# Score and maxima operands in float32r, four tiles of 32 rows, heads 2 and 3 first in the maxima

## What is computed

```python
x = x + 0.5 * moe(layernorm(x), ...)      # 8 experts, top 2, capacity 1280, gelu
x = x + attention(layernorm(x), ...)
x = x + 0.5 * moe(layernorm(x), ...)

def attention(x):                         # B=4, S=1024, H=16, Dh=8
    q, k, v = (split(x @ w.T + b) for w, b in ((wq, bq), (wk, bk), (wv, bv)))
    scores = einsum('bhsd,bhtd->bhst', q, k) / 8 ** 0.5
    weights = softmax(where(causal, scores, -inf), axis=-1)
    return merge(einsum('bhst,bhtd->bhsd', weights, v)) @ wo.T + bo
```

## Time and profile before

| | us |
|---|---|
| time, median of 3 runs (lowest, highest) | 1033.29 (1031.57, 1038.26) |
| span of the profiled execution | 1036.6 |
| TensorE matmuls busy | 831.8 (80%) |
| VectorE busy | 601.5 (58%) |
| ScalarE busy | 523.4 (50%) |
| GpSimd busy | 489.6 (47%) |
| first mixture of experts, then the attention's prologue from | 236 |
| first score at | 289.55 |
| 16 groups of heads until about | 823 |
| last mixture of experts until the end, from | 858 |

### The profile page before, as it was taken

One profiled execution on the slowest core, in us unless ns is written; L12 is line 12 of the kernel. 1 busy time (PEld: TensorE's weight loads), 2 busy tenths in 40 slices (PEclk: granted clock), 3 DMA queues, 4 the chain that ended last, 5 costly groups with the idle time before them and its releaser, 6 DMA issues. The chain is left out here.

```text
span 1036.6 us, 18080 instructions
## 1 busy us (share of the span) xinstructions
PE 831.8 (80%) x6599; PEld 446.5 (43%) x6599; DVE 601.5 (58%) x1237; ACT 523.4 (50%) x841; POOL 489.6 (47%) x686
## 2 busy tenths in 40 slices
PE   8569999944668988888978899878887618999990
PEld 7437878742212223332333323323232316787770
DVE  7931211124767788888787977878775423334235
ACT  6323343442237776777556786566766303433330
POOL 5047455325652662646467522562224651545453
PEclk9769999986657999999799999999899758999995
DMA  7115575621451262341524224323202124423236
GB/s 204 73 26 153 148 217 145 192 63 51 130 162 66 53 189 48 89 144 43 174 76 105 99 53 152 85 65 106 53 18 79 53 63 149 130 79 97 78 136 228
DMA packets 96185, 110.81 MB, mean 107 GB/s; under 512 B 12279, under 2 KB 68763, under 8 KB 96104
## 3 DMA queue, kind: packets, MB, share of 16 engines
q1 hardware_dynamic: 84752, 88.86, 29.1%
q0 software_dynamic: 9216, 17.98, 6.8%
q10 hardware_dynamic: 2136, 2.91, 0.8%
HBM read 57.86 MB, written 52.89 MB: 107 GB/s over the span
## 5 line engine op out<-in xcount | busy, mean ns | idle before, releaser
L1903 DVE TENSOR_REDUCE m_blk<-banks 128x8 f32<-128x1024 f32 (+1 forms) x320 | 348.5, 1114 | 79.7 <-PE banks L1505 67.1
L1823 ACT ACTIVATE pt<-banks 128x1024 f32<-128x1024 f32 (+3 forms) x384 | 300.4, 811 | 145.1 <-PE banks L1489 142.7
L1537 PE MATMUL banks<-pt,vs 128*32 128x512 f32 (+3 forms) x1536 | 176.6, 534 | 7.2 <-POOL pt L2252 3.8
L1489 PE MATMUL banks<-qb,kp 64*128 64x512 bf16 (+3 forms) x768 | 132.6, 351 | 53.7 <-DVE m_blk L1903 45.2
L2252 POOL TENSOR_SCALAR_AFFINE_SELECT pt<-pt 128x512 f32<-128x512 f32 x128 | 81.6, 637 | 192.1 <-ACT pt L1823 191.7
L1505 PE MATMUL banks<-kp,qa 64*128 64x128 bf16 (+4 forms) x1152 | 126.4, 294 | 19.6 <-ACT pt L1823 11.6
L849 POOL DMA_INDIRECT xe<-xn_rows,slot_tok x80 | 79.9, 999 | 94.4 <-PE banks L1190 37.2
L675 POOL DMA_INDIRECT y_tab<-ys,ids x70 | 68.0, 972 | 81.5 <-DVE ys L635 64.5
L1106 ACT ACTIVATE he<-banks,b_up 128x512 f32<-128x512 f32 (+1 forms) x96 | 57.9, 616 | 89.9 <-PE banks L1190 89.5
L1505 PEld LDWEIGHTS banks<-kp,qa 48*128 48x128 bf16 (+1 forms) x1152 | 46.2, 99 | 130.3 <-ACT pt L1823 92.7
L585 ACT ACTIVATE hT<-banks,bfc 128x512 f32<-128x512 f32 (+1 forms) x96 | 56.3, 615 | 84.9 <-DVE bfc L607 48.8
(11 more groups left out here) (344 smaller groups left out, 1128.8 us busy)
## 6 DMA issues: line engine op xcount, KB each, us to landing
bucket<-zero SPq DMA_DIRECT2D x16, 660.0 KB
qb<-q_stack SPq DMA_DIRECT2D x32, 192.0 KB, 3.5
qa<-q_stack SPq DMA_DIRECT2D x30, 192.0 KB, 3.3
kp<-k_stack SPq DMA_DIRECT2D x30, 192.0 KB, 4.2
q_stack<-qp SPq DMA_DIRECT2D x18, 256.0 KB
k_stack<-kq SPq DMA_DIRECT2D x18, 256.0 KB
y_slots<-ye SPq DMA_DIRECT2D x16, 256.0 KB, 2.5
mid<-x SPq DMA_DIRECT2D x8, 512.0 KB, 3.6
```

Of the source, the lines that this page charges most:

```text
L1489: i = nc.tensor.matmul(ring[SLOT["score", 2 * u + pair]][:, s, 0:w], kp[g][rows_s, pair, kb * P:(kb + 1) * P], qb[par][rows_s, pair, q0:q0 ...
L1537: i = nc.tensor.matmul(o_bank[VW * h:VW * h + VW, q:q + w], vs[par][:, kb, h, :], pt[u % PTS][:, h, 0:w], start=u in (0, SECOND), stop=u i ...
L1823: nc.scalar.activation(pt[u % PTS][:, 2 * pair:2 * pair + 2, 0:w], ring[SLOT["score", 2 * u + pair]][:, :, 0:w], ACT.Exp, scale=SCALE).the ...
L1903: nc.vector.tensor_reduce(dst, ring[slot][:, :, 0:blocks * P].rearrange("p s (j k) -> p s j k", k=P), AX.X, ALU.max).then_inc(m_done, 1)
```

## The change

q and k are cut into two float32r parts instead of three bf16 parts, so three products of parts make 24 rows per head instead of 48, in words of four bytes. A head then takes a tile of 32 rows, and the four heads of a group lie on rows 0, 32, 64 and 96 (HR = 32) rather than two and two on the same rows. The second and third parts' steps go: the remainder that VectorE forms is the second part. Maxima are cut into two float32r parts in two steps by GpSimd; the rows that they meet in `kp` hold -1 rather than 1, in place of the negation. Loads of stacks and of maxima are one transfer per head (4) instead of one per 64 rows (2), stores of stacks 3 for each of q and k instead of 6. In the list of maxima units the pair of heads 2 and 3 comes ahead of heads 0 and 1, so M0 is of heads 2 and 3 and M1 of heads 0 and 1.

```diff
-    Q_PART = [0, 0, 0, 1, 1, 2]
-    K_PART = [0, 1, 2, 0, 1, 0]
+    Q_PART = [0, 0, 1]
+    K_PART = [0, 1, 0]
+    HR = 32
...
-            for pair in range(2):
+            for pair in (1, 0):
                 MUNITS.append((hf, pair, segs, row, col, False))
...
-            qa = [sba(f"qa{i}", [P, HS // 2, S], bf16) for i in range(2)]
-            qb = [sba(f"qb{i}", [P, HS // 2, S], bf16) for i in range(2)]
-            kp = [sba(f"kp{i}", [P, HS // 2, S], bf16) for i in range(NG)]
+            qa = [sba(f"qa{i}", [P, S], f32r) for i in range(2)]
+            qb = [sba(f"qb{i}", [P, S], f32r) for i in range(2)]
+            kp = [sba(f"kp{i}", [P, S], f32r) for i in range(NG)]
...
-            parts = [[sba(f"{n}{j}", [P, S], bf16) for j in range(3)] for n in ("qp", "kq")]
-            rest = sba("rest", [P, 2, 512])
+            parts = [[sba(f"{n}{j}", [P, S], f32r) for j in range(2)] for n in ("qp", "kq")]
...
-                    for s in range(2):
-                        sp.dma_start(dst(s), src[s]).then_inc(done, 16)
+                    for h in range(HS):
+                        sp.dma_start(dst[HR * h:HR * h + KS, :].bitcast(f32), src[h]).then_inc(done, 16)
...
-                    for s in range(2):
-                        src = max_rows[hf * 3 * HS:(hf + 1) * 3 * HS, :].rearrange("(c i s) n -> s c i n", c=3, s=2)[s]
-                        dst = qb[par][64 * s + KS:64 * s + KS + 3]
-                        sp.dma_start(dst[:, :, hf * HALF:(hf + 1) * HALF], src).then_inc(max_ld[hf][par], 16)
+                    for h in range(HS):
+                        src = max_rows[hf * 2 * HS:(hf + 1) * 2 * HS, :].rearrange("(c h) n -> h c n", c=2)[h]
+                        dst = qb[par][HR * h + KS:HR * h + KS + 2, hf * HALF:(hf + 1) * HALF]
+                        sp.dma_start(dst.bitcast(f32), src).then_inc(max_ld[hf][par], 16)
...
                     for s in range(2):
-                        rows_s = slice(64 * s, 64 * s + 64)
+                        h = 2 * pair + s
+                        rows_h = slice(HR * h, HR * h + HR)
                         i = nc.tensor.matmul(ring[SLOT["score", 2 * u + pair]][:, s, 0:w],
-                                             kp[g][rows_s, pair, kb * P:(kb + 1) * P],
-                                             qb[par][rows_s, pair, q0:q0 + w], start=True, stop=True)
+                                             kp[g][rows_h, kb * P:(kb + 1) * P],
+                                             qb[par][rows_h, q0:q0 + w], start=True, stop=True)
...
                         for s in range(2):
-                            rows_s = slice(64 * s, 64 * s + (64 if diag else KS))
+                            h = 2 * pair + s
+                            rows_h = slice(HR * h, HR * h + (HR if diag else KS))
                             i = nc.tensor.matmul(ring[slot][:, s, at:at + blocks * P],
-                                                 qa[par][rows_s, pair, qt * P:(qt + 1) * P],
-                                                 kp[g][rows_s, pair, kb * P:(kb + blocks) * P],
+                                                 qa[par][rows_h, qt * P:(qt + 1) * P],
+                                                 kp[g][rows_h, kb * P:(kb + blocks) * P],
                                                  start=not diag or j == 0, stop=not diag)
...
-                        if g == 1 and not bt.final and u in (6, 7, 8, 10):
-                            k = (6, 7, 8, 10).index(u)
-                            second_part(at[("q0", "q1", "k0", "k1")[k]], k // 2, k % 2, k % 2)
...
-                    step(nc.gpsimd.tensor_scalar(m_neg[:], m_of[hf][:], -1.0, None, ALU.mult))
-                    step(nc.gpsimd.tensor_copy(mp[:, 0], m_neg[:]))
-                    step(nc.gpsimd.tensor_tensor(m_neg[:], m_neg[:], mp[:, 0], ALU.subtract))
-                    step(nc.gpsimd.tensor_copy(mp[:, 1], m_neg[:]))
-                    nc.gpsimd.tensor_tensor(mp[:, 2], m_neg[:], mp[:, 1], ALU.subtract).then_inc(parts_ok, 1)
...
+                    nc.gpsimd.tensor_copy(mp[:, 0], m_of[hf][:]).then_inc(p_chain, 1)
+                    wait_apart(pool, p_chain, k + 1)
+                    nc.gpsimd.tensor_tensor(mp[:, 1], m_of[hf][:], mp[:, 0], ALU.subtract).then_inc(parts_ok, 1)
```

More of the change, by code:

```diff
@@ L1347, in store_pieces @@
                 stack, order = ((q_stack, Q_PART), (k_stack, K_PART))[which]
-                for j in range(3):
-                    eng.wait_ge((part_one, rest_ok, split_ok)[j], 3 + which)
+                for j in range(2):
+                    if j == 0:
+                        eng.wait_ge(part_one, 3 + which)
+                    else:
+                        eng.wait_ge(c_evac, pro_at[("q1", "k1")[which]] + 1)
                     for c in range(len(order)):
@@ L1352, in store_pieces @@
                             dst = stack[0:NH * KS, :].rearrange("(h c d) n -> c h d n", h=NH, d=DH)[c]
-                            eng.dma_start(dst[h0:h1], parts[which][j][h0 * DH:h1 * DH, :]).then_inc(done, 16)
+                            eng.dma_start(dst[h0:h1], parts[which][j][h0 * DH:h1 * DH, :].bitcast(f32)).then_inc(done, 16)
             @block.sync
@@ L1757, in take_max @@
                     wait(act, max_st, 16 * k)
-                    take(use, m_rows[hf][:], m_bank[0:MR, 0:P])
+                    take(use, m_rows[hf][:], c_bank[0:MR, 0:P])
                 def take_o(n, hf, read):
@@ L1780, in norm_task @@
                         first_part(at[name], b, "qk".index(name[0]), half, bank_of(at, name))
-                def second_part(use, which, half, slot):
-                    s = slice(half * 512, half * 512 + 512)
-                    act.wait_ge(c_evac, use + 1)
-                    nc.scalar.copy(parts[which][1][:, s], rest[:, slot, :]).then_inc(rest_ok, 1)
                 def out_take(at, name):
@@ L1862, in stack_take @@
                 def stack_take(half, which):
-                    for i in range(PAIRS):
-                        act.wait_ge(st_full, 2 * PAIRS * half + PAIRS * which + i + 1)
-                        dst = (qa[0], kp[0])[which][:, i, half * 512:half * 512 + 512]
-                        nc.scalar.copy(dst, ST_BANK[half][which][i]).then_inc(st_evac, 1)
+                    act.wait_ge(st_full, 2 * half + which + 1)
+                    dst = (qa[0], kp[0])[which][:, half * 512:half * 512 + 512]
+                    nc.scalar.copy(dst, ST_BANK[half][which]).then_inc(st_evac, 1)
                 for half in range(2):
```

149 lines of the change are left out of this document (62 added, 87 removed).

## The result

The changed kernel takes 1188.38 us (median of four, 1181.48 to 1191.39) against 1035.78 us (1031.57 to 1039.57). The ratio is 1.148 (95% interval 1.142 to 1.154), slower by some 153 us. The forecast was 1055 us with a range to 1095, so the direction came true and the size did not: the loss is seven times the forecast one.

A forecast was written before the change was run, and what follows sets the result against it. Bound: a loop in which TensorE's score weight loads and VectorE's maxima reductions wait for each other. 1036.6 + 26 - 3.7 - 0.9 = 1058 us on the span, 1055 us as timed; range 1022 to 1095.

The forecast's parts named there:

- What the new type does to it: Score and maxima matmuls: number and columns stay, rows per head fall, wider float32r weights cost 0.08 us a start.
- a turn: Loop of TensorE and VectorE, one second score pair to the next: 3.04 us, said to become 3.2.
- The dearer starts: TensorE starts with a 128-column weight load in the open: 0.08 us more each, adding 13.4, 4.3 and 2.7 us.
- S1 to V: Start of second score pair to start of value matmuls: from 0.32 us to 0.40 for 512 columns.
- M1 to S0: Start of second maxima unit to start of next first score pair: still 0.23 us or less.
- The diagonal units: Units loading new weights every 128 columns: 0.18 us more each, 60 units, half on the path, 5.4 us.
- the 4.6 that come off: Savings: half of ScalarE's dropped casts, 3.7 us, and GpSimd's shorter first split of the maxima, 0.9 us.
- The first rival: TensorE's float32r weight loads cost no more than bf16, so only savings remain: 1029 us; chance 0.17.
- The half-rate case: TensorE streams float32r at half the rate of bf16; mostly outside the range; 0.13 in the chance of slower.
- Four heads at once: First score and maxima pairs stream together on different row quarters: 9.2 us more off, 1020 us; chance 0.10.
- Maxima late: Two more maxima transfers per half group stand before the scores needing them: 23 us more, 1078 us; chance 0.05.
- The order of the pairs: Maxima of heads 2 and 3 ahead of heads 0 and 1 in each unit: put at nothing.

The follow-up runs named there:

- float32r on 64 rows: Changed kernel's float32r with everything computed, but each head on a 64-row tile, rows 0 to 31 zero, loads and maxima in two transfers: 1075.0 us, ratio 1.042.
- the exchange of the order: Only the order of head pairs in the list of maxima exchanged: in the changed kernel 1191.0 us, in the kernel before 1034.1 us.

## Why the prediction was wrong

**The step that failed** is in "What the new type does to it": the rows per head "fall from 64 (48 used) to 32 (24 used)", named there and then priced at nothing. All terms are worked out at the clock of the earlier trace rows, 1.00, as if it came with the place and not with the work. Fewer rows are not less time for a matmul, and that much is right: with the clock up a turn is 3.04 us on 32 rows of bf16 as on 64. But with half of the rows at work the granted clock falls (0.93 to 0.70 of the sweep, with nothing else moved), and at the low clock a turn is 4.33. No rival held it.

What the runs put in its place: float32r on 64 rows costs 40 us (1075.0 against 1034.5), and going from 64 rows to 32 another 113 (1188.4 against 1075.0). The second can be worked out from the rows. At the low clock are 447 us of the changed kernel's sweep and 2 x 0.08 x 565.3 = 90 us of the float32r kernel's on 64 rows, 357 us more. Of each such microsecond (4.71 - 3.24) / 4.71 = 0.31 would not be there at the full clock: 111 us, where the two sweeps differ by 677.5 - 565.3 = 112. So of the 153 us about 40 came in the way that was forecast, and the direction would have come true with these alone; the larger part came by a way that the prediction did not have.

**The dearer starts** came as described and were mis-sized. Weights of 128 columns load in 196 ns (170 to 200 was said), and the loads that wait stand in the loop. That the sum has no term for the streaming itself was an assumption, for which the trace before has nothing. The float32r kernel on 64 rows bears it out: a pair is two records, one per head, and S0 to M0 is 0.23 us for 512 columns (411.02 to 411.25) against 0.22 in bf16. The size was 0.08 us a start; S1 to V went from 0.32 to 0.42 and M1 to S0 from 0.23 to 0.34, so up to 0.11. The diagonal units were taken at 0.18 us; from their matmuls to the mask's it went from 0.33 (421.69 to 422.02) to 0.60 (422.90 to 423.50), 0.27. With these, 168 x 0.11 + 54 x 0.11 + 34 x 0.11 + 30 x 0.27 = 36 us instead of 26; less the 4.6 that come off, 32. The float32r kernel on 64 rows lies 40 us above the kernel before by its runs and 29.5 by its profiled span, which is that of its fastest run; its sweep is 565.3 - 527.5 = 38 us longer, but starts 7 us earlier. M1 to S0, said to stay at 0.23, is 0.34 (410.68 to 411.02). S0's loads stand at 410.79, beside M1, and S0 to M0 has hardly grown (0.22 to 0.23), so what grew there is M1's own start. The forecast's own upper end, 1076 us, comes to 1077 from its terms; nothing hangs on it.

**The first rival** (starts no dearer) fell with the loads' 196 ns: float32r goes with the f32 loads (192) and not with bf16 (95). The half-rate case, 0.13 in the chance of slower, was the author's assumption. No run shows float32r streaming at half the rate of bf16: S0 to M0 is 0.23 us against 0.22, as above, and S1 to V 0.42. **Four heads at once** was right in that the pairs stream together: S0 and M0 start 0.01 us apart, and so do their loads (525.18 and 525.19). The gain that it named, in units that wait for no reduction, can't be read out of a sweep that is mostly at the low clock; which pair overlaps makes no difference, as the exchange of the order shows. The overlap is seen two pairs at a time, and the step from 64 rows to 32 that brings it costs 113 us.

**Maxima late** did not come. The wait for them in the first group, 5.02 us at 305.38, is now

```profile
304.07 0.80 PE L1496 MATMUL banks<-qb,kp 32*128 32x512 f32 x2 [2.63 <-DMA qb<-max_rows]
```

and later scores do not wait for this transfer. (The prediction read that none did before; one load of scores waited 0.6 us for it.) The halved stores of the stacks may have a part in it, for which the prediction put nothing:

```profile
283.84 2.62 SPq L1359 DMA_DIRECT2D q_stack<-qp  x3
286.50 4.43 SPq L1359 DMA_DIRECT2D k_stack<-kq  x3
```

They take 7.05 us of issue, where the earlier trace rows had 8.4; no run changes them alone. **The order of the pairs** was put at nothing, and the two experiments on it bear that out within 1%. What ScalarE's missing casts are worth by themselves was not tried.

## What to carry to other kernels

Before the tiles of TensorE's main matmuls get smaller, ask how many rows of the array will be at work over time, and give the clock a term of its own: the price of a lower clock on the whole loop, turn by turn, as a rival at least. Rows of zeros beside the used ones did not lengthen the matmuls (0.49 us for a pair of 512 columns at the full clock, 0.50 on 32 rows), and here they were worth 113 us. A wider word in the weights costs at each start whose load is in the open, about 0.11 us here; find these starts and count them.

## What was unexpected of the hardware

Zero rows count: the clock is 0.92 in the sweep with half of each 64-row tile zero, and 0.93 with all of it filled. So what counts here is how many rows take part, and not the numbers in the added ones. TensorE busy for 92% of a stretch by the records (40.46 of 44 us) had the low clock throughout. Each kind of matmul gone to 32 rows lowers the mean clock of the sweep on its own (0.84, 0.83), both further (0.70). And on 32-row tiles the records show a matmul ahead of an earlier one on other rows: at 403.19 us M1 and the next M0, four matmuls, stream together, while S0, which stands between them in the program on M1's rows, starts at 403.78. Whether the engine or the record changes the order, no run here tells.
